# The order of steps in opening, body and closing laid anew, for a fused graph convolution, linear attention and mixture of experts on one core

## What is computed

```python
x = x + conv(_gn(x), ...)      # per batch: lhs, rhs -> 16x16 softmax E over time; x_tat = x E;
                               # lhs2, rhs2 -> 256x256 softmax S; sum over 3 cheb: (cheb[k]*S) x Theta[k]
                               # relu, 1x3 convolution over time, + residual (x rw), relu, LayerNorm over 16
t = _to_tokens(x)              # (16, 256 tokens, 256)
t = t + attn(_ln_t(t), ...)    # q, k, v; elu+1; causal linear attention, 16 heads of 16; Wo
t = t + ffn(_ln_t(t), ...)     # shared silu(gate)*up -> down (512 wide), and 16 experts of 64,
                               # 4 chosen of 2 of 4 groups, weighted, all experts computed
```

## Time and profile before

| | us |
|---|---|
| median of 3 runs | 938.91 |
| lowest, highest | 932.68, 941.02 |
| the profiled execution: its time | 936.66 |
| the profiled execution: its span | 934.8 |

### The profile page before, as it was taken

One profiled execution on the slowest core, in us unless ns is written; L12 is line 12 of the kernel. 1 busy time (PEld: TensorE's weight loads), 2 busy tenths in 40 slices (PEclk: granted clock), 3 DMA queues, 4 the chain that ended last, 5 costly groups with the idle time before them and its releaser, 6 DMA issues.

```text
span 934.8 us, 19500 instructions
## 1 busy us (share of the span) xinstructions
PE 882.2 (94%) x7856; PEld 783.3 (84%) x7856; DVE 620.9 (66%) x1629; ACT 434.5 (46%) x843; POOL 230.1 (25%) x198
## 2 busy tenths in 40 slices
...
PEclk9999799999999999999999999999999999999999
...
GB/s 234 1 1 1 129 66 1 47 72 24 24 27 70 34 26 12 72 36 24 23 13 84 23 35 24 26 72 20 39 13 49 59 1 23 31 77 25 33 71 34
DMA packets 36105, 39.21 MB, mean 42 GB/s; under 512 B 3248, under 2 KB 32432, under 8 KB 36016
## 3 DMA queue, kind: packets, MB, share of 16 engines
...
HBM read 32.97 MB, written 4.98 MB: 41 GB/s over the span
## 4 chain that ended last, share of the span: by engine, by line
PE 82%; DVE 8%; ACT 4%; issue 3%; DMA 2%; POOL 1%; SPq 0%; POOLq 0%; DVEq 0%
PE ring L1361 8%; PE g_ps L517 5%; PE d_ps L517 5%; PE g_ps L519 4%; PE g_ps L518 4%; PE u_ps L517 4%; PE u_ps L519 4%; PE u_ps L518 4%; PE d_ps L519 4%; PE d_ps L518 4%; PE ring L1229 4%; PE num L1258 3%; PE ring L1454 3%; PE ring L1344 3%; PE ring L519 3%
## 5 line engine op out<-in xcount | busy, mean ns | idle before, releaser
L701 POOL TENSOR_TENSOR hl<-hb,hh 128x512 fp32r<-128x512 f32 x96 | 126.5, 1318 | 404.7 <-ACT hh L839 404.7
L839 ACT ACTIVATE hh<-hb 128x512 fp32r<-128x512 f32 x96 | 60.6, 632 | 177.3 <-DVE hb L1201 165.0
L517 PE MATMUL d_ps<-hh,down_h 128*128 128x256 f32 x384 | 114.7, 299 | 3.3 <-POOL hl L701 3.2
L1196 DVE TENSOR_TENSOR hb<-sl,u_ps 128x512 f32<-128x512 f32 x88 | 60.1, 683 | 79.5 <-PE u_ps L519 36.3
L517 PE MATMUL g_ps<-normed_h,gate_h 128*128 128x256 f32 x352 | 106.6, 303 | 3.4 <-DVE hb L1196 3.4
L518 PE MATMUL d_ps<-hl,down_h 128*128 128x256 f32 x384 | 107.7, 280 | 0.0
L519 PE MATMUL d_ps<-hh,down_l 128*128 128x256 f32 x384 | 107.5, 280 | 0.0
L519 PE MATMUL g_ps<-normed_h,gate_l 128*128 128x256 f32 x352 | 99.8, 283 | 0.0
L518 PE MATMUL g_ps<-normed_l,gate_h 128*128 128x256 f32 x352 | 99.3, 282 | 0.0
L519 PE MATMUL u_ps<-normed_h,up_l 128*128 128x256 f32 x352 | 99.2, 282 | 0.0
L518 PE MATMUL u_ps<-normed_l,up_h 128*128 128x256 f32 x352 | 99.0, 281 | 0.0
...
## 6 DMA issues: line engine op xcount, KB each, us to landing
weights_over_hidden<-weights_by_expert SPq DMA_DIRECT2D x128, 128.0 KB, 3.0
...
```

Of the source, the lines that this page charges most:

```text
L517: eng.matmul(ps, wh, xh, start=start, stop=False, **how)
L701: pool.tensor_tensor(hl[:, j % 2, :], hb, hh[:, j % 2, :].bitcast(F32), ALU.subtract).then_inc(*ffn_pool.mark(p, f"lo{j}"))
L839: act.activation(hh[:, j % 2, :], hb, ACT.Copy).then_inc(*ffn_act.mark(p, f"hi{j}"))
L1196: dve.tensor_tensor(hb, sl, gate_up(p, j)[1][:, :], ALU.mult).then_inc(*ffn_dve.mark(p, f"h{j}"))
```

## The change

The three tables have the same words in another order. No function, size, buffer or wait call is edited. Two pairs of lines of the tables, as the diff has them (the second line of OPENING, the first of BODY), and the last of BODY:

```diff
 OPENING = """
...
-    0:hot4 0:Eexp 0:high1 0:hot5 1:Y0 1:prod 2:xg 1:Epre 0:Erep 0:lr 0:hot6 1:Eexp 0:high2 2:xT0 0:p2 1:Erep 2:M 1:lr
...
+    1:Y0 0:Eexp 1:prod 0:high0 2:xg 0:Erep 1:Epre 2:xT0 0:lr 1:Eexp 2:M 1:Erep 0:p2 1:lr 2:xT1 0:low0 0:sp0 0:rv0 0:xb
...
 BODY = """
-    +1 tok0 lg +1 gn tok1 +3 nrm xg +2 r1 xl0 +1 xT0 xl1 M +2 xT1 r2 k0 k1 v1 q0 v0 r3 +2 Y0 silu +1 r4 prod cb Epre
...
-    Y1 +1 V10 st1 o0 o1 xb tc0 tc1 z1 +1 S11 +3 V11 +1 at1 z2 +1 wo0 wo1 +1 tk0 +3 tk1 +4 nrm2 z3 +1 xn0 xn1 +1 exp +1
+    +1 tok0 tok1 lg +1 gn +4 nrm xg +1 xl0 xl1 +1 r1 xT0 M r2 xT1 +2 k0 k1 v1 r3 +2 Y0 +1 prod silu r4 q0 v0 cb Epre
...
+    V01 xb +2 S10 +2 tc0 tc1 +1 V10 +1 S11 +3 z1 V11 +1 at1 z2 +2 wo0 wo1 +2 tk0 tk1 +4 nrm2 z3 +2 xn0 xn1 exp +1
```

More of the change, by code:

```diff
@@ L124 @@
-    0:v1 0:q0 0:v0 0:kt 0:q1 0:high4 2:p2 0:hot15 0:hot16 0:high5 0:dent 0:kv 0:rd 0:low2 0:high6 0:S00 0:hot17
-    0:high7 2:sp0 0:V00 0:S01 0:hot18 0:high8 0:hot19 0:low3 0:low4 0:at0 0:high9 2:rv0 0:hot20 0:V01 0:S10 0:hot21
-    2:sp1 2:st0 0:V10 0:low5 0:S11 2:rv1 0:low6 0:hot22 0:V11 0:high10 0:at1 2:Y1 0:high11 0:wo0 0:wo1 0:hot23 0:tk0
-    0:tk1 0:nrm2 2:st1 2:o0 0:xn0 0:xn1 0:low7 1:tok0 1:tok1 0:low8 0:lg 0:r1 1:nrm 0:r2 0:low9 0:low10 +2 2:o1 +1
-    2:xb 0:r3 1:xl0 1:xl1 2:tc0 +1 0:low11 0:high12 0:silu 0:low12 0:high13 0:r4 1:k0 +1 1:k1 1:v1 1:q0 +1 0:cb 1:v0
@@ L129 @@
-    1:kt +3 1:q1 +2 2:tc1 +1 0:low13 1:dent +2 1:kv +1 1:rd +2 1:S00 +4 0:exp 1:V00 +2 2:z1 1:S01 +2 1:at0 +2 1:V01 +1
-    1:S10 +3 1:V10 +1 1:S11 +1 1:V11 +1 2:z2 1:at1 +2 2:z3 +1 1:wo0 1:wo1 +3 1:tk0 1:tk1 +4 1:nrm2 +2 1:xn0 1:xn1
-    1:exp +1
+    0:hot0 0:gn 0:xg 0:hot1 0:hot2 0:xT0 1:gn 1:xg 0:M 0:xT1 1:xT0 0:hot3 1:M 0:hot4 0:Y0 1:xT1 2:gn 0:prod 0:Epre
+    1:Y0 0:Eexp 1:prod 0:high0 2:xg 0:Erep 1:Epre 2:xT0 0:lr 1:Eexp 2:M 1:Erep 0:p2 1:lr 2:xT1 0:low0 0:sp0 0:rv0 0:xb
+    1:p2 0:sp1 0:st0 1:sp0 0:hot5 0:rv1 0:hot6 1:rv0 0:Y1 0:hot7 1:sp1 1:st0 0:st1 0:low1 0:high1 0:o0 0:o1 2:Y0
@@ new lines @@
+    0:hot8 1:rv1 0:tc0 2:prod 0:tc1 0:z1 1:Y1 0:z2 0:hot9 0:high2 2:Epre 1:st1 0:z3 1:o0 2:Eexp 1:o1 0:tok0 0:high3
+    0:tok1 1:tc0 1:tc1 0:hot10 0:hot11 0:hot12 1:xb 0:nrm 0:hot13 1:z1 0:hot14 2:Erep 0:low2 0:xl0 0:xl1 2:lr 0:hot15
+    1:z2 0:k0 1:z3 0:k1 0:v1 0:q0 0:v0 0:kt 0:high4 0:q1 2:p2 0:hot16 0:dent 0:kv 0:low3 0:rd 0:S00 0:hot17 2:sp0
+    0:V00 0:S01 0:low4 0:high5 0:low5 0:high6 0:hot18 0:hot19 0:hot20 0:at0 2:rv0 0:high7 0:V01 0:high8 0:S10 0:hot21
+    2:sp1 2:st0 0:low6 0:V10 0:S11 0:low7 0:hot22 0:V11 2:rv1 2:Y1 0:at1 0:wo0 0:wo1 0:high9 0:hot23 0:high10 0:high11
@@ L132 @@
+    0:tk0 0:tk1 0:nrm2 2:st1 0:low8 0:high12 2:o0 0:xn0 0:low9 0:low10 0:low11 0:xn1 2:o1 1:tok0 1:tok1 2:xb 2:tc0
+    1:nrm +2 1:xl0 +1 1:xl1 0:lg 0:r1 0:r2 +2 1:k0 1:k1 0:r3 1:v1 +1 0:silu +1 0:r4 +2 1:q0 0:cb 1:v0 1:kt 1:q1 +2
+    0:low12 +1 1:dent +1 1:kv +1 0:high13 +1 0:low13 1:rd 1:S00 +2 2:tc1 0:exp +1 1:V00 +1 1:S01 +1 1:at0 +1 1:V01 +2
+    1:S10 +1 1:V10 +4 1:S11 +3 1:V11 +1 2:z1 1:at1 +4 2:z2 2:z3 +2 1:wo0 1:wo1 +2 1:tk0 1:tk1 +5 1:nrm2 +1 1:xn0 1:xn1
+    +1 1:exp
 """
 BODY = """
-    +1 tok0 lg +1 gn tok1 +3 nrm xg +2 r1 xl0 +1 xT0 xl1 M +2 xT1 r2 k0 k1 v1 q0 v0 r3 +2 Y0 silu +1 r4 prod cb Epre
@@ L138 @@
 """
 CLOSING = """
-    +1 7:tok0 7:tok1 +2 7:nrm +3 6:lg +1 6:r1 +1 7:xl0 7:xl1 6:r2 +1 6:r3 6:silu +1 6:r4 +2 7:k0 7:k1 7:v1 7:q0 6:cb
-    7:v0 7:kt 7:q1 +3 7:dent 7:kv +2 7:rd +1 7:S00 +2 7:V00 7:S01 7:at0 +1 7:V01 +1 7:S10 +4 7:V10 7:S11 +1 7:V11 +1
-    7:at1 +1 7:wo0 +2 7:wo1 7:tk0 7:tk1 +4 7:nrm2 +2 7:xn0 +6 7:xn1 +4 7:lg 7:r1 +4 7:r2 +2 7:r3 7:silu +2 7:r4 +3
-    7:cb +16 7:exp +29
+    7:tok0 7:tok1 +1 6:lg +6 7:nrm 6:r1 +1 7:xl0 7:xl1 6:r2 +1 6:r3 +2 6:silu 6:r4 7:k0 +1 7:k1 7:v1 7:q0 6:cb 7:v0
```

9 lines of the change are left out of this document (4 added, 5 removed).

## The result

The changed kernel takes 955.77 us in the median of 4 runs (954.33 to 956.42), the kernel before 938.97 beside it: a ratio of 1.0188, with 95% certainty between 1.0139 and 1.0238. The forecast was 926 us with a range up to 937. The change makes the kernel 17 us slower, and the prediction was wrong in its sign.

A forecast was written before the change was run, and what follows sets the result against it. PE was taken as the bound, busy 882.2 of 934.8 us. Opening -8.3, body -2.7 and closing +0.5 sum to -10.5 us against the profiled 936.66, giving 926.2; forecast 926, range 917 to 937.

The forecast's parts named there:

- the opening: Up to pair 0's first ffn round: earlier steps fill PE's gaps, 8.3 us gained, between 0 and 15.3.
- the body: Five turns: 5.2 us of waits gone, 2.5 of new ones, net 2.7 us gained, between 0 and 5.2.
- the closing: The end, V01 of pair 7 and S10 behind S01: +0.5 us, between -1 and +2.
- Pair 0's chain in the opening: Erep ahead of Epre and earlier steps in gaps gain 3.4 us; Y0 of pair 2 ahead of tc0 gains 2.1.
- the 4 asked: Sign in the opening: tok0 of pair 0 starts at least 4 us sooner.
- The gap behind tc1 of pair 1: Opening: five hot steps in PE's 3.13 us wait keep the clock up, 1.2 us gained, between 0 and 2.7.
- The first ffn round: End of the opening: o1 and tc0 of pair 2 cover waits ahead of gu0, net 1.6 us gained, between 0 and 2.3.
- The wait of xl0: First ffn round: pair 1's xl0 comes sooner behind its LayerNorm and waits about 0.7 us.
- the new waits: Body: 0.5 us a turn, 2.5 in all, about half of what is taken away.
- The gains at gu1 and S11: Body: gu1's wait for h0 gains 2.9 us, S11's wait for tc1's relu 2.3, sum 5.2.
- the three dangers that were named: Body: zq1 awaited by dent, p2 close behind lr's ACT copies, z1 ahead of at1 on DVE; new waits 2.5 us.
- the slower rival: Turns: at1 late behind z1, DVE operations stretched beside POOL passes; 5 us a turn, 951 us; chance 0.1 with other losses.

The follow-up runs named there:

- hots_more: Changed kernel with 29 hot steps (busy matmuls with no result) in place of 24, two moved later and five added in the opening: 952.9 us, ratio 1.0168.
- gap_hots: Kernel before with six more hot steps in the opening, five behind tc1 of pair 1 and one ahead of lg of pair 0: 933.6 us, ratio 0.9959.
- tok_first: Changed kernel with tok0, tok1 and nrm of pair 1 ahead of o1 of pair 2, tk0 and tk1 one gu step later, in the opening's table: 954.1 us.
- nrm_only: Changed kernel with nrm right behind h0 and ahead of w0 in the body, tk0 and tk1 left: 945.8 us, one run.
- tk_only: Changed kernel with tk0 and tk1 one gu step later in the body, nrm left: 956.3 us, one run.
- old_closing: Changed kernel with the closing order of the kernel before: 950.2 us, ratio 1.0113.
- old_opening: Changed kernel with the opening order of the kernel before: 947.9 us, ratio 1.0107.
- body_nt: Changed kernel with two moves in the body, nrm right behind h0 and tk0 and tk1 one gu step later: 950.2 us, ratio 1.0131.
- old_body: Changed kernel with the body order (inside the turns) of the kernel before: 950.1 us, ratio 1.0130.
- turn_two: Kernel before with tok1 beside tok0 ahead of lg, and S11 one gu step later, in a turn: 938.6 us, ratio 0.9997.
- half2: Kernel before with about the second half of a turn's new order, tk0 and tk1 one gu later, p2 directly behind lr: 961.8 us, ratio 1.0263.
- repaired: Changed kernel with tok_first, nrm_only and old_closing together: 942.7 us, ratio 1.0057.

## Why the prediction was wrong

Forecast were -8.3 us for the opening, -2.7 for the body and +0.5 for the closing. Measured, with the same steps in both, are +6.7, +6.1 and +6.7. The sum failed in its durations, which it took at the clock of the kernel before, and in the covers that the moved steps took from others, which it missed or put too low in the first ffn round, in the turns and in the closing.

**Pair 0's chain in the opening** (forecast -3.4 and -2.1; measured up to tok0 of pair 0: +2.1). This step failed. Its order was right in kind: Erep stands ahead of Epre, Y0 of pair 2 waits 0.8 us in place of 2.64, and in hots_more, at full clock, tok0 comes 3.9 us sooner, about the 4 asked. But the sum took every duration from the earlier trace rows at the clock of the kernel before. It counted the hot steps only where they were put and not where they were taken from, and M of pair 1, which had filled 20.4 to 23.2 us, at nothing. In the change Erep starts at 29.31 us, 0.3 sooner and not 1.9. Y0 of pair 1 ahead of it takes 2.09 us in place of 1.17, which is 0.9 of the missing 1.6; in hots_more, at full clock, Erep starts at 28.45, so the clock isn't all of it:

```profile
25.89 2.09 PE L1243 MATMUL ring<-theta_s,raw_weights 32*128 32x128 f32 x32 [0.57 <-DVE shared L940]
29.31 1.89 PE L1317 MATMUL ring<-iw,shared 16*128 16x17 f32 x8 [0.27 <-ACT kept L744]
```

**The gap behind tc1 of pair 1** (-1.2). Right in kind, and too small: between tok0 and S00 of pair 0 the change makes up 2.4 us, and the wait of 3.13 us is 1.01 with the clock at 1.00. The whole 2.7 us, which the prediction gave as the result of the clock rule in the Trainium skill (TensorE: Matmul & The Clock Gate, Part 1: the HAM clock gate), was the nearer number. gap_hots bears it out in the other kernel.

**The first ffn round** (-1.6; measured +3.0 up to the end of gu1). Failed. The wait of xl0 was seen and put at 0.7; it is 2.14, for tok1 of pair 1 now stands behind the 5-us product while its LayerNorm, up to the end of L794, takes 5.8 us from there, and 6.8 us at half clock follow. After that, tk0 of pair 1 waits 2.74 us at 240 us, which the prediction didn't cost at all. To take these two away isn't enough, as tok_first shows: with both gone, the second gu0 comes 0.3 us sooner.

**The body** (-2.7; measured +7.5, of which 1.8 is lg of pair 6). Failed: the new waits were put at half of what was taken away, without a row for any of them. The gains at gu1 and S11 came (5.7 us less in the list of waits, 5.2 forecast), the three dangers that were named (kv and dent, p2, at1 behind z1) did not show, and the loss came at two steps that were not looked at. At xl0, w0 had gone ahead of nrm, and POOL's pass with it; at tk0, gu9 (2.9 us) stood between wo1 and tk0, and now dn8 (1.4 us) does, with a held L1019 on DVE ahead of the residual sum. nrm_only gives the first back, and with it all but 0.6 us of what the body lost. tk_only takes the second wait away and gets nothing for it. At both places stands the mechanism of the slower rival, a DVE operation of 0.15 to 0.2 us that ends with a whole pass of POOL, about 1 us a turn each in place of 5. How much of each wait it makes, beside the places of the steps, no run tells apart. The rival named the sign and a mechanism that is there, though not where it priced it, and its chance of 0.1 was too small.

**The closing** (+0.5; measured +4.9, with lg of pair 6 +6.7, and 5.6 by old_closing). Failed: only S01 to S10 was looked at. The trace has 3.4 us at half clock from 887 us and small waits (0.4 at xn0, 0.2 at lg) around it. The stretch is worth about 1.5 us: from gu0 of pair 6 to that of pair 7 the change takes 87.1 us, and four kernels with the same closing whose profiles lack the stretch (old_opening, body_nt, nrm_only, tk_only) take 85.6. Which of the moved steps makes the rest was not tried.

**The chances.** Each gain was read from a wait that stands in the trace of before, and each loss had to come from a wait that doesn't stand there. In the turns half of what was removed was allowed for these; the runs say that it is all of it: in nrm_only neither gu1 nor S11 waits any more, and its five turns take 547.2 us, with 4.8 us of waits at tk0 in their place, where the old body, in which both wait, takes 547.0; turn_two takes 546.0 for 546.2. That there was little to win was to be seen in the earlier trace rows: only 2.1 us of a turn of 109 are without a matmul.

**Open.** Why the opening's table still costs 7 us at the second gu0 when xl0 and tk0 wait no more. The largest part shows in the granted clock. The table sets PE's work at half clock up to the end of the second gu0 beside that end; the last column takes off half of it, which is an estimate:

| | opening | second gu0 ends | PE's work at half clock | less half of it |
|---|---|---|---|---|
| before | before | 248.7 | 15.8 | 240.8 |
| half2 | before | 246.9 | 9.2 | 242.3 |
| turn_two | before | 255.7 | 33.4 | 239.0 |
| gap_hots | before and fill | 245.3 | 6.8 | 241.9 |
| change | changed | 255.8 | 24.5 | 243.6 |
| old_body | changed | 257.2 | 33.4 | 240.5 |
| hots_more | changed and fill | 256.6 | 25.6 | 243.8 |
| tok_first | repaired | 255.5 | 20.9 | 245.1 |
| repaired | repaired | 255.6 | 26.8 | 242.2 |

So 4.3 of the change's 7.1 us and 5.5 of repaired's 6.9 go with the half clock, and turn_two is as late with the opening of before. The changed opening has more half-clock time in most of its profiles, but which of its steps makes the clock fall behind 88 us no run shows. The rest lies in waits for DVE (hb, pairs), which has the same instructions, later; lg, which starts some 10 us later, and the three splits ahead of xn1 are candidates, and no run moved them alone.
